# End of the last batch: down products behind all gates, the two halves in turn, and the last step of the second half with tokens on partitions

## The reference, cut to what matters

```python
x = hidden_states.reshape(-1, H)              # per batch here: 512 tokens x 128
def expert_step(acc, w):
    wg, wu, wd = w                             # 128x512, 128x512, 512x128
    h = jax.nn.silu(x @ wg) * (x @ wu)
    return (acc + h @ wd, None)
acc, _ = jax.lax.scan(expert_step, zeros, (Wg, Wu, Wd))      # 8 experts
...
x = x + _layernorm(_L0_ffn_ref(_layernorm(x), Wg, Wu, Wd))   # mean and variance over 128 features, per token
```

## Time and profile before

| What | Value |
|---|---|
| Median of three runs | 543.49 us |
| Profiled execution: time, recorded span | 543.36 us, 541.6 us |
| TensorE busy | 535.0 us, 99% of the span |
| TensorE weight loads busy | 466.7 us, 86% |
| VectorE, ScalarE, GpSimd busy | 441.1, 348.1, 167.9 us |
| Granted TensorE clock | 1.000 of full, the level of 2.4 GHz, over the whole span |
| Last matmul of the down products, start | 535.75 us |
| Last store issued | 539.55 us |

### The profile page before, as it was taken

The page is one execution under the profiler, slowest core; times in us unless marked ns, Lnnn a source line. Parts: engine busy times, 40 slices in busy tenths (PEclk is TensorE's granted clock), DMA queues, the critical chain, the costliest instruction groups (busy, mean ns, idle before and its releaser), DMA issues.

```text
span 541.6 us, 8642 instructions
## 1 busy us (share of the span) xinstructions
PE 535.0 (99%) x2577; PEld 466.7 (86%) x2577; DVE 441.1 (81%) x968; ACT 348.1 (64%) x632; POOL 167.9 (31%) x217
## 2 busy tenths in 40 slices
PE   9999999999999999999999999999999999999996
PEld 6788888888888888888888888888888888888886
DVE  7886877899777997879977898688987799777866
ACT  5986877557684565856667566765767555655555
POOL 5796950217102280114602145021530016000101
PEclk9999999999999999999999999999999999999999
DMA  6354111120220201202102111021111110110000
GB/s 199 107 166 112 47 59 50 30 78 20 60 71 9 97 24 36 79 20 79 57 3 79 40 59 59 7 72 39 60 39 48 31 61 0 41 39 1 20 2 19
DMA packets 33798, 28.68 MB, mean 53 GB/s; under 512 B 3412, under 2 KB 25687, under 8 KB 33751
## 3 DMA queue, kind: packets, MB, share of 16 engines
q1 hardware_dynamic: 32736, 27.47, 16.1%
q10 hardware_dynamic: 1014, 0.66, 0.4%
HBM read 17.37 MB, written 10.75 MB: 52 GB/s over the span
## 4 chain that ended last, share of the span: by engine, by line
PE 98%; ACT 1%; issue 0%; DVE 0%; POOLq 0%; POOL 0%; DVEq 0%; ACTq 0%
PE acc_att_ps L1217 11%; PE acc_att_ps L1216 11%; PE acc_att_ps L1219 11%; PE gate_ps L1216 10%; PE gate_ps L1217 10%; PE gate_ps L1219 10%; PE up_ps L1217 10%; PE up_ps L1216 10%; PE up_ps L1219 10%; PE acc_att_ps L1262 1%; PE up_ps L1333 1%; ACT xh L800 0%; PE acc_att_ps L1277 0%; PE acc_att_ps L1268 0%; PE acc_att_ps L1274 0%; PE acc_att_ps L1378 0%
## 5 line engine op out<-in xcount | busy, mean ns | idle before, releaser
L734 ACT ACTIVATE gs<-gate_ps 128x512 f32<-128x512 f32 x255 | 152.1, 597 | 172.9 <-PE gate_ps L1219 170.4
L1014 DVE TENSOR_TENSOR h<-gs,up_ps 128x512 f32<-128x512 f32 x231 | 157.5, 682 | 76.4 <-PE up_ps L1219 66.7
L1001 DVE TENSOR_TENSOR h_lo<-h,h_hi 128x512 fp32r<-128x512 f32 x231 | 170.5, 738 | 0.1
L711 ACT ACTIVATE h_hi<-h 128x512 fp32r<-128x512 f32 x231 | 144.1, 624 | 6.8 <-DVE h L1014 5.4
L1216 PE MATMUL gate_ps<-x1nT_hi,wg_hi 128*128 128x512 f32 (+1 forms) x254 | 98.4, 388 | 0.0
L1216 PE MATMUL acc_att_ps<-h_hi,wd_hi 128*128 128x512 f32 (+1 forms) x256 | 96.9, 378 | 0.0
L1217 PE MATMUL acc_att_ps<-h_hi,wd_lo 128*128 128x512 f32 (+1 forms) x256 | 96.9, 378 | 0.0
L1219 PE MATMUL acc_att_ps<-h_lo,wd_hi 128*128 128x512 f32 (+1 forms) x256 | 96.9, 378 | 0.0
L1216 PE MATMUL up_ps<-x1nT_hi,wu_hi 128*128 128x512 f32 (+1 forms) x254 | 96.1, 378 | 0.0
L1217 PE MATMUL gate_ps<-x1nT_hi,wg_lo 128*128 128x512 f32 (+1 forms) x254 | 96.1, 378 | 0.0
L1217 PE MATMUL up_ps<-x1nT_hi,wu_lo 128*128 128x512 f32 (+1 forms) x254 | 96.1, 378 | 0.0
(11 more groups left out here) (266 smaller groups left out, 554.7 us busy)
## 6 DMA issues: line engine op xcount, KB each, us to landing
w_raw<-in_L_ffn_Wg_dram SPq DMA_DIRECT2D x8, 256.0 KB, 3.0
w_raw<-in_L_ffn_Wu_dram SPq DMA_DIRECT2D x8, 256.0 KB, 2.8
w_raw<-in_L_ffn_Wd_dram SPq DMA_DIRECT2D x8, 256.0 KB, 2.9
x_in<-in_L_attn_x_dram SPq DMA_DIRECT2D x7, 256.0 KB, 2.8
t_dram_x1n<-t_blk_x1n SPq DMA_DIRECT2D x7, 256.0 KB, 2.0
t_out_x1n<-t_dram_x1n SPq DMA_DIRECT2D x28, 64.0 KB, 1.9
t_dram_acc<-t_blk_acc SPq DMA_DIRECT2D x7, 256.0 KB, 2.3
t_out_acc<-t_dram_acc SPq DMA_DIRECT2D x28, 64.0 KB, 2.1
```

The source lines that it names most:

```text
L711: act.activation(h_hi[s % NH][:, :], h_of(t, s)[:, :], ACT.Copy).then_inc(s_hhi, 1)
L734: act.activation(gs[q][:, :], gate_ps[q][:, :], ACT.Silu).then_inc(s_silu, 1)
L1001: dve.tensor_tensor(h_lo[s % NH][:, :], h_of(t, s)[:, :], h_hi[s % NH][:, :].bitcast(F32), ALU.subtract).then_inc(s_hlo, 1)
L1014: dve.tensor_tensor(h_of(t, s)[:, :], gs[q][:, :], up_ps[q][:, :], ALU.mult).then_inc(s_h, 1)
```

## The change

1. TensorE, last batch: the down products of steps 26 and 27, which stood between the gates of steps 29, 30 and 31, now stand behind the last gates. Behind them come step 28 at full width, then steps 29, 30 and 31 for the first half into `att_ps`, and steps 29 and 30 for the second half into `acc_ps`.
2. Step 31 of the second half isn't added there. Its blocks of `h_hi` and `h_lo` become the stationary operand and Wd the moving one (128 columns), so that the result has tokens on partitions; `accT`'s transposed second half is added in the same bank.
3. To make the sum lie by halves, every down product of the last batch (`t >= (B - 1) * STEPS`) reads `h` in a row instead of in pairs. The copy to `accT` reads a plain half.
4. The copy at L836 goes. ScalarE and VectorE make `h_hi` and `h_lo` of step 30 behind the silu and the product of step 31.
5. The tail works in three groups: tiles 0 and 1, tile 2, tile 3 (`LAST_TILES`); GpSimd raises to the power three times.

```diff
+        LAST_TILES = (slice(0, 2), slice(2, 3), slice(3, 4))
+        def acc_half(i):
+            return acc_ps[:, (HALF, REST)[i]]
+
+        def h_in_order_of_acc(v, t):
+            return v if t >= (B - 1) * STEPS else pairs(v)
+
+        def tile_of(v, j):
+            return v.rearrange("p (i t j) -> p i j t", i=2, j=JH)[:, j // JH, j % JH]
...
-            for i, toks in enumerate(halves):
-                power("fin", B - 1 + i * JH + JH, s_rstd["fin"], s_mv["fin"], toks)
+            for toks in LAST_TILES:
+                power("fin", B - 1 + toks.stop, s_rstd["fin"], s_mv["fin"], toks)
...
-                h_hi_of(t - 1, s - 1, False)
                 act.wait_ge(s_h, t - since(s, NGU) + 1)
                 for i, half in enumerate((HALF, REST)):
                     act.wait_ge(s_gate, t + 1 + i)
                     act.activation(gs[q][:, half], last_gate_ps[i][:, half], ACT.Silu).then_inc(s_silu, 1)
+                h_hi_of(t - 1, s - 1, False)
                 act.wait_ge(s_down, t - since(s, NH) + 1)
...
-            act.wait_ge(s_down, B * STEPS - 2)
-
             for i, half in enumerate((HALF, REST)):
-                act.activation(accT[:, half], acc_ps[:, :].rearrange("p (c i) -> p i c", i=2)[:, i],
-                               ACT.Copy).then_inc(s_last_acc, 1)
-
-            act.wait_ge(s_res, B - 1)
-            act.wait_ge(s_down, B * STEPS)
-            act.activation(last_sum[:, REST], last_acc_ps[1][:, REST], ACT.Copy).then_inc(s_last_copy, 1)
+                act.wait_ge(s_down, B * STEPS - 3 if i == 0 else B * STEPS)
+                act.activation(accT[:, half], acc_half(i), ACT.Copy).then_inc(s_last_acc, 1)
...
-                products(acc_ps[:, :], w_hi[2][:, e, cols], w_lo[2][:, e, cols], pairs(h_hi[q][:, :]), pairs(h_lo[q][:, :]),
-                         s == 0, last or s == STEPS - 1, s_hlo, t + 1).then_inc(s_down, 1)
+                products(acc_ps[:, :], w_hi[2][:, e, cols], w_lo[2][:, e, cols], h_in_order_of_acc(h_hi[q][:, :], t),
+                         h_in_order_of_acc(h_lo[q][:, :], t), s == 0, last or s == STEPS - 1, s_hlo, t + 1).then_inc(s_down, 1)
...
+                for k in (5, 4, 3):
+                    down(t - k, s - k, False, last=(k == 3))
...
+                for k in (2, 1, 0):
+                    last = down_half(k, 0, att_ps[:, HALF], k == 2, k == 0)
+                last.then_inc(s_down, 1)
+
+                pe.wait_ge(s_last_acc, 1)
+                for k in (2, 1):
+                    down_half(k, 1, acc_half(1), False, k == 1).then_inc(s_down, 1)
+
+                pe.wait_ge(s_acc, B)
+                for j in range(JH):
+                    pe.transpose(last_banks[j][:, 0:P], tile_of(last_sum, j), ident[:, :]).then_inc(s_last_T, 1)
+
+                pe.wait_ge(s_hhi, t + 2)
+                pe.wait_ge(s_hlo, t + 2)
+                for j in range(JH, J):
+                    pe.matmul(last_banks[j][:, 0:P], tile_of(h_hi[r][:, :], j), w_hi[2][:, e, cols], start=True, stop=False)
+                    pe.matmul(last_banks[j][:, 0:P], tile_of(h_hi[r][:, :], j), w_lo[2][:, e, cols], start=False, stop=False)
+                    pe.matmul(last_banks[j][:, 0:P], tile_of(h_lo[r][:, :], j), w_hi[2][:, e, cols], start=False, stop=False)
+                pe.wait_ge(s_last_acc, 2)
+                for j in range(JH, J):
+                    pe.matmul(last_banks[j][:, 0:P], tile_of(accT[:, :], j), ident[:, :], start=False,
+                              stop=True).then_inc(s_last_T, 1)
...
-                    if s >= LAG:
+                    if s >= LAG and not (last and s >= STEPS - 3):
```

More of the change, by code:

```diff
@@ L351, in build @@
         s_last_acc = sem("s_last_acc")
-        s_last_copy = sem("s_last_copy")
         s_last_nm = sem("s_last_nm")
@@ L1194, in _ @@
             dve.wait_ge(s_last_acc, 1)
-            dve.wait_ge(s_down, B * STEPS - 1)
-            dve.tensor_tensor(last_sum[:, HALF], last_acc_ps[0][:, HALF], accT[:, HALF], ALU.add).then_inc(s_acc, 1)
-            for i in range(2):
-                for j in range(i * JH, i * JH + JH):
+            dve.wait_ge(s_down, B * STEPS - 2)
+            dve.tensor_tensor(last_sum[:, HALF], att_ps[:, HALF], accT[:, HALF], ALU.add).then_inc(s_acc, 1)
+            for toks in LAST_TILES:
+                for j in range(toks.start, toks.stop):
                     dve.wait_ge(s_last_T, j + 1)
                     dve.bn_stats(st["fin"][:, j, 0:6], last_banks[j][:, 0:D]).then_inc(s_st["fin"], 1)
-                for j in range(i * JH, i * JH + JH):
+                for j in range(toks.start, toks.stop):
                     dve.wait_ge(s_st["fin"], B + j)
@@ L1301, in last_step @@
                                  pairs_of(x1nT_lo[par][:, :], i), True, True, s_x1nT_lo, B).then_inc(s_done, 1)
-                down(t - 3, s - 3, False)
-                down(t - 2, s - 2, False, last=True)
-                for i, half in enumerate((HALF, REST)):
-                    ps = last_acc_ps[i]
-                    for k in (1, 0):
-                        r, e, f = (s - k) % NH, (s - k) // FT, (s - k) % FT
-                        cols = slice(f * D, f * D + D)
-                        made = t if k else t + 1 + i
-                        pe.wait_ge(s_hhi, made)
-                        last = products(ps[:, half], w_hi[2][:, e, cols], w_lo[2][:, e, cols], h_hi[r][:, half],
-                                        h_lo[r][:, half], k == 1, k == 0, s_hlo, made)
-                    last.then_inc(s_down, 1)
+                for k in (5, 4, 3):
+                    down(t - k, s - k, False, last=(k == 3))
@@ new lines, in down_half @@
+                def down_half(k, i, ps, start, stop):
+                    e, f, r, half = (s - k) // FT, (s - k) % FT, (s - k) % NH, (HALF, REST)[i]
+                    cols = slice(f * D, f * D + D)
+                    made = t - k + 1 + (i if k == 0 else 0)
+                    pe.wait_ge(s_hhi, made)
+                    pe.matmul(ps, w_hi[2][:, e, cols], h_hi[r][:, half], start=start, stop=False, skip_group_check=True)
+                    pe.matmul(ps, w_lo[2][:, e, cols], h_hi[r][:, half], start=False, stop=False, skip_group_check=True)
+                    pe.wait_ge(s_hlo, made)
+                    return pe.matmul(ps, w_hi[2][:, e, cols], h_lo[r][:, half], start=False, stop=stop,
+                                     skip_group_check=True)
@@ new lines, in last_step @@
+                e, f, r = s // FT, s % FT, s % NH
+                cols = slice(f * D, f * D + D)
+                pe.wait_ge(s_hhi, t + 2)
[4 more added lines that the diff above has]
+                    pe.matmul(last_banks[j][:, 0:P], tile_of(h_lo[r][:, :], j), w_hi[2][:, e, cols], start=False, stop=False)
@@ L1324, in body @@
                         down(t - LAG, s - LAG, first)
-                    elif not first:
+                    elif not first and s < LAG:
                         down(t - LAG, STEPS + s - LAG, False)
```

24 lines of the change are left out of this document (5 added, 19 removed).

## The result

| | before | changed |
|---|---|---|
| Median (runs) | 543.52 us (10) | 544.94 us (10) |
| Lowest to highest | 543.3 to 544.26 | 544.53 to 545.37 |
| Profiled execution: time, span | 543.36, 541.6 | 544.53, 542.7 |
| Last store issued | 539.55 | 540.68 |

What follows compares the result with a forecast made beforehand. TensorE's stream was taken to bound the kernel up to the last down product, then a chain of small operations. +0.56 for reading in a row and -0.13 at the tail made +0.43, so 543.9 us, range 543.2 to 544.9.

Steps and rivals of the forecast that it cites:

- Step 4: Last batch's 87 full down matmuls reading in a row: 0.0064 us more each, +0.56 us, ends -0.20 and +1.11.
- per column: Rival, 15%: reading in a row costs 0.0128 us per full down matmul of the last batch, giving 544.47.
- Free at full width: Rival, 24%: reading in a row costs nothing at 512 columns, only the tail's gain counts, giving 543.36.
- pairs are what is slow: Rival, 3%: by the cacheline rule, reading in a row speeds the last batch's down matmuls up, giving 543.2.
- Step 1: TensorE before the tail: one full down product becomes half-wide matmuls, so the sum on VectorE comes 0.29 us earlier.
- Does TensorE wait: End of last batch: h_lo of step 31's first half ready 0.33 us before TensorE asks; the reordering costs nothing.
- Step 2: Tail, tiles 2 and 3: six 128-column matmuls of step 31, one pass of 0.118 us each, 0.71 us in all.
- two-pass rival: Rival, 13%: tail's 128-column fp32r matmuls take two passes, six cost 0.71 us more; 544.5, or 545.0 with per-column cost.
- Step 3: Tail, three powers on GpSimd for two: last multiply-add starts at 539.04 instead of 539.17, a gain of 0.13 us.

Runs made afterwards that it cites:

- e1: Changed kernel, but down products of batches 0 to 7 read their moving columns in eight different orders, output not the reference's; 591.53 us.
- e2: Kernel before, with only the full down products of the last batch (90 matmuls) reading in a row; 544.98 us, ratio 1.0026.
- e3: Changed kernel, but the last batch's down products read pairs inside each half of the tokens instead of in a row; 543.36 us, ratio 0.9991 to before.
- e6: e3 with the down products of steps 26 and 27 back between the gates, new ScalarE and VectorE order kept; 543.82 us, ratio 1.0003 to before.
- e9: e3 with both the place of steps 26 and 27 and the ScalarE and VectorE order as before; 543.56 us, ratio 0.9998 to before.
- e5: e3 with the tail's tiles 2 and 3 sharing statistics and power again, two powers for three; 543.24 us, ratio 0.9994 to e3.
- e4: Like e1, with two streams 64 down to 2 elements apart, then eight and four streams; output not the reference's; 580.14 us.
- e8: e3 with steps 26 and 27 behind all gates, but ScalarE and VectorE in their old order in the last step; 544.18 us, ratio 1.0008 to before.

## Why the prediction was right and wrong

- **Step 4, reading in a row: wrong in its reason and in size, and it decided.** The direction and the place were right (all 87 full matmuls, all on TensorE's path). The term was 0.0064 each, +0.56; measured are 0.015 each, +1.30 (0.017 in e1 and e2). What failed is the step from the half-wide row to the full one: "a cost per weight change and so per matmul". The half-wide matmuls cost 0.0064 to 0.007 and those of twice the width 0.015 to 0.017, so it goes by columns as far as two widths can show it, and even a little more. The rival "per column" had 15% and said 0.0128 and 544.47; its own condition for being slower by over 0.2%, 0.014 each, was met. The upper bound of the term, 0.0128, was also too low.
- What the profile held against my choice: the full matmul had 0.1 us to spare over a weight load, so a cost that stems from the weights should have vanished at 512 and not stayed the same. Only nothing or per column fitted; the value between them fitted neither.
- **"Free at full width"** (24%) and "pairs are what is slow" (3%) are refuted by e1 and e2.
- **Step 1: right.** -0.29 worked out. In e3, where the pace is undisturbed, the sum comes 0.33 earlier although its batch began 0.02 late (472.05 against 472.03); of this 0.35, 0.06 is the half-wide matmuls' faster pace.
- **Does TensorE wait: right, for this kernel.** The copy of step 30 did wait for step 26's product (the ScalarE row above). `h_lo` of step 31's first half was done at 535.35 + 0.42 = 535.77, and TensorE asked for it at 536.15: 0.38 of slack, 0.33 worked out. But "costs nothing" said less than was there. The move and the new order together remove a gap that halves of three steps would otherwise have, worth 0.45 (e6) or 0.31 (e9) with the start of the batch taken off; I had compared only with the kernel before, which has halves of two.
- **Step 2: right.** One record for each of L1335 to L1337, about 0.118 apart from the second on (537.46, 537.58). The two-pass rival (13%) is out. The pace of 81 ns that the Trainium skill gives for 128 columns ("TensorE: Matmul & The Clock Gate", section "Back-to-back issue gap") is not seen here. In the sum by that pace GpSimd is free at 536.87 + 0.71 = 537.58, not at 537.55 as written; nothing hangs on it.
- **Step 3: the tail was forecast 0.14 too long.** Taken were -0.29 at the sum and -0.13 at the end, so 0.16 lost between; measured is 0.02 (4.11 against 4.09). The powers of one column run at 1.07 / 2 = 0.53 as estimated, but without the slowing by VectorE for which I had added up to 0.13. That VectorE was the reason for it isn't shown: beside its multiply-adds a power of two columns took 0.83 in the kernel before and 0.74 in e5. And VectorE began its multiply-adds 2.82 behind the sum (539.39 - 536.57) and not 2.97 (538.14 - 535.17), a little before the record of tile 3's `bn_aggr` ends (539.27 + 0.20).
- **The sum.** Forecast +0.56 - 0.13 = +0.43. Measured at the last store: +1.30 - 0.29 + 0.02, and 0.11 with which the batch began late, = +1.14 (1.13 read).
- **The range.** Its upper end, 544.9, came from the two-pass case, which didn't happen; the per-column case, the nearest to what did, ended at 544.47. That the median missed the range by only 0.04 is luck.

## What to carry to other kernels

The order in which TensorE reads its moving operand has a price of its own (seen here for fp32r). Where a layout forces another order, look for one that keeps two alternating streams and still gives the layout, and pay for it with a stride in the copy out of PSUM. A cost that is seen at one width only should be carried to another as nothing or per column, with both as cases, and not as a value between them. And a move that "costs nothing" against the old kernel may still be what keeps another part of the same change from waiting; undo the parts in pairs. Before a difference of a few tenths between two single traces is put down to a change, compare where the changed stretch begins: here two executions differed by up to 0.66 before they reached it.

## What was not expected of the hardware

For 512-wide fp32r matmuls at the full clock: two alternating streams at least 4 elements (16 bytes) apart 0.216 us, in a row 0.233, runs of two from two streams 0.33, four streams 0.28, every second element 0.447, eight streams 0.53. A count of the 16-byte lines touched (see e4) doesn't give this series: two, four and eight streams touch the same lines equally often. Runs of four elements from two streams (0.25) are slower than a plain row, though they too take four elements from a line in turn. What the mechanism is stays open. Reads of 256 columns of PSUM with a stride of two elements cost nothing more in ScalarE's copy and VectorE's sum (0.39 and 0.42 us either way). And a wait of TensorE costs its length and 0.1 us besides, since the next matmul follows at 0.21 instead of 0.11 (e6, e8, e9).
